# A mixture of experts after an attention block: expert outputs added straight into the output tensor, gates gathered with the rows

## The reference

```python
mod = (silu(c) @ wmod).reshape(4, 6, 1, -1)
sa, ca, ga, sb, cb, gb = (mod[:, i] for i in range(6))
ga = (2*(ga >= 0) - 1) * maximum(abs(ga), 0.25)      # gates, one row of 256 per sequence
gb = (2*(gb >= 0) - 1) * maximum(abs(gb), 0.25)
x = x + ga * attention(layernorm(x) * (1 + ca) + sa)  # 16 query heads, 4 key/value heads of 16
h = layernorm(x) * (1 + cb) + sb
x = x + gb * experts(h)
# experts: probs = softmax(h @ router.T); of 8 experts a token keeps the likeliest ones up to
# a total of 0.9; out = sum over kept e of w[e] * ((silu(h @ gate[e].T) * (h @ up[e].T)) @ down[e].T)
```

## Time and profile before

| | us |
|---|---|
| median of 3 runs (613.22, 614.0, 616.6) | 614.0 |
| the profiled execution, its own time | 614.37 |
| its span, first to last instruction | 612.6 |
| PE busy | 483.4 (79%) |
| DVE busy | 371.3 (61%) |
| ACT busy | 282.5 (46%) |
| POOL busy | 170.9 (28%) |
| mean granted clock of TensorE | 0.894 of full speed |

### The profile page before, as it was taken

The page is one execution under the profiler, slowest core; times in us unless marked ns, Lnnn a source line. Parts: engine busy times, 40 slices in busy tenths (PEclk is TensorE's granted clock), DMA queues, the critical chain, the costliest instruction groups (busy, mean ns, idle before and its releaser), DMA issues. The chain is left out here.

```text
span 612.6 us, 10534 instructions
## 1 busy us (share of the span) xinstructions
PE 483.4 (79%) x3498; PEld 351.2 (57%) x3499; DVE 371.3 (61%) x910; ACT 282.5 (46%) x409; POOL 170.9 (28%) x184
## 2 busy tenths in 40 slices
PE   2745978898899789997315599999997998999810
PEld 2333323244344433425215599999997998999810
DVE  4496287669936983567678175665643755465526
ACT  0244669776886788782000244453423543443300
POOL 6104000000000000000000336656665556476440
PEclk9965989998999999987655699999998998999975
DMA  8243100000000010010121134636453446333338
GB/s 291 95 135 117 61 1 1 1 0 2 24 13 1 1 35 1 1 35 1 34 73 35 46 104 98 158 60 164 90 125 61 109 98 151 56 52 60 44 37 271
DMA packets 33815, 42.01 MB, mean 69 GB/s; under 512 B 5620, under 2 KB 26868, under 8 KB 33784
## 3 DMA queue, kind: packets, MB, share of 16 engines
q0 software_dynamic: 10400, 16.22, 14.5%
q1 hardware_dynamic: 23384, 25.39, 13.0%
HBM read 28.14 MB, written 13.46 MB: 68 GB/s over the span
## 5 line engine op out<-in xcount | busy, mean ns | idle before, releaser
L511 ACT ACTIVATE probs<-psS 128x1024 f32<-128x1024 f32 x128 | 124.0, 1023 | 16.3 <-PE psS L1162 16.0
L1340 PE MATMUL psS<-hs_hi,w_hi 128*128 128x256 f32 x400 | 117.5, 294 | 6.9 <-issue 3.9
L1340 PE MATMUL psS<-hs_lo,w_hi 128*128 128x256 f32 x400 | 114.4, 286 | 0.0
L1340 PE MATMUL psS<-hs_hi,w_lo 128*128 128x256 f32 x400 | 114.3, 286 | 0.0
L404 POOL DMA_INDIRECT y_rows<-y_sel,idx_out x50 | 83.4, 1668 | 55.3 <-DVE y_sel L1035 45.0
L1340 PEld LDWEIGHTS psS<-hs_hi,w_hi 128*128 128x128 f32 x400 | 77.5, 194 | 8.4 <-issue 7.7
L1162 PE MATMUL psS<-qT,kT 96*128 96x512 bf16 x256 | 71.7, 393 | 11.1 <-ACT probs L511 9.4
L1340 PEld LDWEIGHTS psS<-hs_lo,w_hi 128*128 128x128 f32 x400 | 77.7, 194 | 0.0
L1340 PEld LDWEIGHTS psS<-hs_hi,w_lo 128*128 128x128 f32 x400 | 77.5, 194 | 0.0
L1271 PE MATMUL psY<-probs,v_aug 128*32 128x512 f32 x512 | 70.8, 626 | 0.0
L369 POOL TENSOR_TENSOR rstd<-var_eps,minus_half 128x4 f32<-128x4 f32 x4 | 4.8, 1195 | 235.2 <-DVE var_eps L764 235.2
(11 more groups left out here) (188 smaller groups left out, 807.6 us busy)
## 6 DMA issues: line engine op xcount, KB each, us to landing
w_in<-gateT SPq DMA_DIRECT2D x8, 512.0 KB
w_in<-upT SPq DMA_DIRECT2D x8, 512.0 KB
w_in<-downT SPq DMA_DIRECT2D x8, 512.0 KB
x_all<-x SPq DMA_DIRECT2D x4, 512.0 KB, 7.9
mod_rows<-mod_table SPq DMA_DIRECT2D x4, 512.0 KB, 7.6
y_rows<-zeros POOLq DMA_DIRECT2D x2, 1024.0 KB
h_rows<-h_nat SPq DMA_DIRECT2D x4, 512.0 KB, 3.0
y_all<-y_rows SPq DMA_DIRECT2D x4, 512.0 KB, 5.7
```

The lines of the kernel that those rows point to most:

```text
L511: act.activation(probs[:, gk % 4, 2 * pair:2 * pair + 2, :], psS[:, pair, :, :], ACT.Exp, scale=ATT_SCALE).then_inc(probs_done, 1)
L1340: mm = pe.matmul(ps[:, i * SW:(i + 1) * SW], w, v[:, k, :], start=at == 0, stop=at == 3 * KC - 1)
```

## The change

- The experts' results are added (scattered) into `out` itself. Therefore SP writes each sequence's `x` after attention into `out` as soon as it stands, behind the write of `h`, and the read-back, the product with `gb`, the sum and the final write at the end are gone, as is the zeroing of `y_rows`.
- The gate `gb` has to be applied before the scatter: `h_rows` gets 256 more numbers per row (520 in all), into which POOL writes the gate rows with four transfers as soon as they are made. A gather brings them along, `take_weights` copies 2x264 numbers instead of 2x8 into a ring of four buffers, and `output` multiplies by weight and gate row in one instruction. `modulate_gates(1)` moves from the end to the end of DVE's body 0.
- Lists are filled with tokens that did not choose the expert (their weight is 0) instead of pad rows: three small operations more in the rank, two fewer after the lists, and no pad rows.
- POOL makes the roots for sequences 2 to 4 first and the routing tables after them. PE waits at its first score for a semaphore of its own (`v_ones`), and the waits for all constants move behind attention.

```diff
@@ sync
                 sp.dma_start(h_rows[bass.ds(b * N, N), 0:C]...).then_inc(h_out, 16)
+                sp.dma_start(out_rows[bass.ds(b * N, N), :].rearrange("(t p) c -> p t c", p=P),
+                             x_all[:, bass.ds(b * TT, TT), :]).then_inc(x2_out, 16)
...
-            sp.wait_ge(scattered, ZEROING + 32 * items)
-            for b in range(B):
-                sp.dma_start(y_all[:, b * TT:(b + 1) * TT, :],
-                             y_rows[b * N:(b + 1) * N, :].rearrange("(t p) c -> p t c", p=P)).then_inc(y_in[b], 16)
-            for b in range(B):
-                sp.wait_ge(out_ready, b + 1)
-                sp.dma_start(out[b].rearrange("(t p) c -> p t c", p=P), ...).then_inc(y_out, 16)
+            sp.wait_ge(x2_out, 16 * B)
+            sp.wait_ge(scattered, GATES + 32 * items)
@@ gpsimd
-            for m, v in ((v_aug[...], 0.0), (tie, 1.0), (earlier, 1.0), (zeros, 0.0)): memset
+            pool.memset(v_aug[:, :, :, :, D:YROWS], 0.0).then_inc(zeroed, 1)
+            pool.wait_ge(zeroed, 4)
+            pool.memset(v_aug[:, :, :, :, D:D + 1], 1.0).then_inc(v_ones, 1)
+            pool.wait_ge(ln1_eps, 2)
+            pool.tensor_tensor(rstd1[:, TT:], var_eps1[:, TT:], minus_half[:, 0:NT - TT], ALU.pow).then_inc(ln1_rstd, 1)
...          memsets, affine_selects, iota slot_row, slot_tile, token (0-based); no pad_row
-            pool.wait_ge(ln1_eps, 2)
-            pool.tensor_tensor(rstd1[:, TT:], ...)
-            for r0, r1 in ((0, T // 2), (T // 2, T), (T, T + PADS)): zeros to y_rows; zeros to h_rows
+            pool.wait_ge(modr_done, 3)
+            for b in range(B):
+                pool.dma_start(h_rows[b * N:(b + 1) * N, C + E:ROW].rearrange("(t p) c -> p t c", p=P),
+                               mod_rows[:, B + b:B + b + 1, :].broadcast_to([P, TT, C])).then_inc(scattered, 16)
...
-                    pool.indirect_dma_start(y_rows[:, :], ..., y_sel[:, k, :], None, compute_op=ALU.add)
+                    pool.indirect_dma_start(out_rows[:, :], ..., y_sel[:, k, :], None, compute_op=ALU.add)
@@ vector, end of body 0
                     modulate_gates(0, xhat[:, :, :], h_nat[:, :, :])
+                    dve.wait_ge(modr_done, 1)
+                    modulate_gates(1, xhat[:, :, :], h_nat[:, :, :])
                     dve.tensor_scalar(mod_rows[:, SCALE_ROW:, :], ..., 1.0, None, ALU.add).then_inc(modr_done, 1)
@@ vector, routing
+            dve.tensor_copy(token_f[:, :, :], token[:, :, :]).then_inc(token_ready, 1)
...
-            step(dve.tensor_copy(rank_i[:, :, :], rank[:, :, :]))
+            step(dve.tensor_tensor(others[:, :, :], token_f[:, :, :], wide, ALU.add))
+            step(dve.scalar_tensor_tensor(out=others, in0=rank, scalar=-2.0, in1=others, op0=ALU.mult, op1=ALU.add))
+            step(dve.scalar_tensor_tensor(out=others, in0=keep, scalar=0.0, in1=others, op0=ALU.is_equal, op1=ALU.mult))
+            step(dve.tensor_tensor(rank_i[:, :, :], rank[:, :, :], others[:, :, :], ALU.add))
...
-            step(dve.tensor_copy(row_f, row_i)); step(row_f = (row_f + 1) * keep); step(row_h = row_f - 1)
+            step(dve.tensor_copy(row_h[:, :, :], row_i[:, :, :].rearrange("p t e -> p e t")))
...
-            step(is_pad = (lists == 0) * pads); ids_i = lists - 1 + is_pad; idx_all = pad_row - 1
+            dve.tensor_copy(ids_i[:, :, :], lists).then_inc(rt_step, 1)
+            dve.memset(idx_all[:, :], 0).then_inc(idx_ready, 1)
@@ vector, experts
-                dve.tensor_scalar(w_sel[:, bass.ds(m + 1, 1), :, 1:]..., h_sel[:, :, C:ROW], 0.0, None, ALU.max)
+                dve.tensor_scalar(sel[:, bass.ds(m % RING, 1), :, 1:]..., h_sel[:, :, C:ROW], 0.0, None, ALU.add)
...
-                    weighed = dve.tensor_scalar(y_sel[:, k, :], psY[:, k, 0:C], w_sel[...], None, ALU.mult)
+                    weighed = dve.scalar_tensor_tensor(out=y_sel[:, k, :], in0=psY[:, k, 0:C], scalar=row[:, bass.ds(e1, 1)],
+                                                       in1=row[:, 1 + E:], op0=ALU.mult, op1=ALU.mult)
...
-            modulate_gates(1, ...), and for each b: y = y * gate rows (L1072), y = y + x_all (L1074)
```

More of the change, by code:

```diff
@@ L942, in _ @@
             step(dve.tensor_tensor(rank[:, 1:, :], rank[:, 1:, :], total[:, 0:NT - 1, :], ALU.add))
[L943 removed]
+            wide = total[:, NT - 1:NT, :].broadcast_to([P, NT, E])
+            step(dve.tensor_tensor(others[:, :, :], token_f[:, :, :], wide, ALU.add))
+            step(dve.scalar_tensor_tensor(out=others[:, :, :], in0=rank[:, :, :], scalar=-2.0, in1=others[:, :, :],
+                                          op0=ALU.mult, op1=ALU.add))
+            step(dve.scalar_tensor_tensor(out=others[:, :, :], in0=keep[:, :, :], scalar=0.0, in1=others[:, :, :],
+                                          op0=ALU.is_equal, op1=ALU.mult))
+            step(dve.tensor_tensor(rank_i[:, :, :], rank[:, :, :], others[:, :, :], ALU.add))
             step(dve.tensor_scalar(tile_i[:, :, :], rank_i[:, :, :], 7, None, ALU.logical_shift_right))
@@ L946, in _ @@
             step(dve.tensor_copy(tile_h[:, :, :], tile_i[:, :, :]))
-            step(dve.tensor_copy(row_f[:, :, :], row_i[:, :, :]))
-            step(dve.scalar_tensor_tensor(out=row_f[:, :, :], in0=row_f[:, :, :], scalar=1.0, in1=keep[:, :, :],
-                                          op0=ALU.add, op1=ALU.mult))
-            step(dve.tensor_scalar(row_h[:, :, :], row_f[:, :, :].rearrange("p t e -> p e t"), -1.0, None, ALU.add))
+            step(dve.tensor_copy(row_h[:, :, :], row_i[:, :, :].rearrange("p t e -> p e t")))
             dve.wait_ge(h_out, 16 * (B + 1))
@@ L1013, in take_weights @@
                 dve.wait_ge(gathered, 32 * (m + 1))
-                dve.tensor_scalar(w_sel[:, bass.ds(m + 1, 1), :, 1:].rearrange("p o k e -> p (o k) e"), h_sel[:, :, C:ROW], 0.0,
-                                  None, ALU.max).then_inc(w_copied, 1)
+                dve.tensor_scalar(sel[:, bass.ds(m % RING, 1), :, 1:].rearrange("p o k e -> p (o k) e"), h_sel[:, :, C:ROW], 0.0,
+                                  None, ALU.add).then_inc(w_copied, 1)
             def product(m, h):
@@ L1064, in _ @@
             output(E, items - 1)
-            modulate_gates(1, y_all[:, 0:B, :], y_all[:, B:2 * B, :])
-            dve.wait_ge(modr_done, 3)
-            for b in range(B):
-                y, tiles = y_all[:, b * TT:(b + 1) * TT, :], slice(b * TT, (b + 1) * TT)
-                dve.wait_ge(y_in[b], 16)
-                dve.tensor_tensor(y, y, mod_rows[:, B + b:B + b + 1, :].broadcast_to([P, TT, C]), ALU.mult).then_inc(out_step, 1)
-                dve.wait_ge(out_step, b + 1)
-                dve.tensor_tensor(y, y, x_all[:, tiles, :], ALU.add).then_inc(out_ready, 1)
         @block.tensor
```

96 lines of the change are left out of this document (37 added, 59 removed).

## The result

| | before | after |
|---|---|---|
| median of 7 runs each, same chip | 614.6 | 617.8 |
| range | 613.2 to 616.6 | 617.0 to 620.6 |
| profiled execution: its time, its span | 614.4, 612.6 | 618.0, 616.3 |

The ratio is 1.0059, 95% interval 1.0035 to 1.0084: slower by 0.6%, where 601 was forecast. The span is 16.7 us longer than the 599.6 of the sum. Differences between two changed kernels go across chips, on which the kernel before had medians of 614.2 to 615.3; they are good to about 1 us.

What follows compares the result with a forecast made beforehand. PE, nearly always busy in attention and experts, was taken as the bound. End -17.8, start -5.4, gates +5.4, routing +0.3 and experts +4.5 sum to -13.0: span 599.6, median 601 us, range 593 to 610.

Steps and rivals of the forecast that it cites:

- Start, -5.4: Setup: with the tables later, xhat of sequence 1 saves PE 5.8 us; holding sequence 2's xhat costs 0.4.
- Gates, +5.4: DVE's body 0: modulate_gates(1) ahead of normalise_x(2) delays PE by 3.7 us, plus 1.7 for a lower clock.
- Routing +0.3: Routing: three more small operations before the lists, two fewer behind, two fewer in the middle, one copy; net +0.3 us.
- The experts, +4.5: Expert turns: longer gathered rows land later, costing seven tight turns and the first gather; +4.5 us in all.
- The landing: Expert gathers: twice the bytes per row add up to 0.5 us to each landing.
- may hold [the scatter's issue] a little, 0 to 0.3: Experts: the longer take_weights on DVE falls beside POOL's scatter issue and may hold it 0 to 0.3 us.
- What takes the place of the end, +0.2: End of program: after the last scatter only SP's wait for it and one semaphore remain, 0.2 us.
- 1: Whole kernel: the terms hold as summed, 601 us, own range 597 to 606; chance 0.60.
- 5, the other side: Experts: a longer gather issue on POOL sets every item's pace; 613.5 us, or 629 with contention; chance 0.08.
- the danger sign: Experts: PE's waits at h_sel summing to more than 10 us would show the prediction wrong.

Runs made afterwards that it cites:

- `gates_early`: Changed kernel with both modulate_gates and the 1 + scale moved up in DVE's body 0 to right behind normalise_x(1); 608.7 us, ratio 0.9879.
- `copy16`: Changed kernel, gathers of 520 numbers kept, but take_weights copies only 2x8 weights and output uses sequence 0's gate row; 608.6 us, ratio 0.9894.
- `short16`: Changed kernel with gathered rows of 264 numbers, take_weights copying 2x8, and output using sequence 0's gate row; 602.1 us, ratio 0.9798.
- `copy528`: Changed kernel, long rows and 2x264 copy kept, but output multiplies by sequence 0's gate row at a fixed address; 610.5 us, ratio 0.9927.
- `sem_nudge`: Changed kernel with two increments of an unused semaphore on DVE ahead of the first operation of split_weights; 613.8 us, ratio 0.9998.
- `tail`: Changed kernel with POOL's loop running as many turns as there are items, without empty turns; 610.0 us, ratio 0.9928.

## Why the prediction was wrong

- **Start, -5.4:** right (5.3 ahead at PE's first transposes and again from 67 to 104).
- **Gates, +5.4:** right where it was summed. The wait (+4.1) and the half clock behind it made 5.6: the lead of 5.3 was a lag of 0.3 at 152. Another 1.7 came where I did not look, from 3.4 us more at 1.2 GHz at 262. `gates_early` gives both back.
- **Routing +0.3:** the operations that the prediction lists cancel (four more, four fewer), so its sum did not follow from them; the lag grew by 0.4 from 268 to the first list. Lists and `out` as the target: too small to see.
- **The experts, +4.5: the step that failed.** Measured are 13.5 in the turns and 0.8 ahead of them. I had PE's waits at `h_sel` grow by the later landing alone, and let the other engines' order stand. In all 16 profiles the turns last 222.5 to 224.2 us, plus PE's waits at `h_sel`, plus half of the time at 1.2 GHz between the first turn and the last (an estimate from those three rows of each profile); from before to after the waits grow by 10.7 and the half clock by 2.2. Behind that stand three things.
  - The landing: taken as 0.5 later per gather, measured 0.7 to 0.9. Its cost, 4.9 to 6.5 us by `copy16` against `short16`, is near the whole term as summed, which is partly luck: the sum has 6 in the turns for a landing 0.8 later. As an estimate by the Trainium skill (DMA: Bandwidth & Descriptors, Anatomy of one DMA), 131 KB more would have made the landing 0.3 later; the measurement decides.
  - The wide copy: 1.9 in the medians when the rows are long, nothing when they are short.
  - The tie of scatter and split, in no case of mine. `copy528` is 7.3 faster than the changed kernel, but it also takes register operations out of `output`; `sem_nudge` keeps them, has no long issue either, and is 4.1 faster. In the profiles both shorten the turns by 5.5 to 5.7. So the tie costs 4 to 7 us, and where the medians of these two part is open. I wrote that `take_weights` "may hold [the scatter's issue] a little, 0 to 0.3", and looked at durations only. The starts in the trace of before are 0.03 us apart and 0.08 away from the bad side, so any edit to `output` or to POOL's turn could tip the order. The change tipped it with an operand's address.
- **What takes the place of the end, +0.2: failed as well, 4.7 measured.** I took the end of the work for the end of the program. POOL's seven empty turns and the drain were in the trace of before, hidden beneath the 17 us that the change removes; asking what else still ran beneath that stretch would have found them.
- **The cases:** 1 had the right list but not these two; 5, the other side, had the wrong mechanism (the issue of the gather, 1.0 us as before), though its place, the gather's round ahead of the turn, was where the time went. What I called the danger sign, waits at `h_sel` above 10 us, came: 14.0.

What can be tested of the sum: 601 + 4.5 (end) + 0.4 (landing) + 2.1 (up to the first list) = 608.0, and `copy16`, which has these and neither the wide copy nor a long issue, takes 608.6. From there to 617.8 the steps of 1.9 (wide copy) and 7.3 are differences of medians and add up by construction. Shown by experiments: the end, the gates, the landing, the tie as a cause, and that an operand's address tips it. Only argued: the exact size of the tie, whether the wide copy costs 2 us with long rows (the interval of `copy528` overlaps that of `copy16`) and why, and what in DVE's register operations moves by 0.05 us.

## What to carry to other kernels

When an edit removes the last stretch of a program, look at what every other engine's stream still does there, its loops' empty turns and its drain too. Where two engines that disturb each other start within some 0.1 us in the trace, treat their order as a coin: give the loss a chance of its own, and separate them by a wait or by another order of the work. And a wait that ends at a transfer has several releasers in a row (scatter ahead of the gather, then the copy behind the split): moving the first alone gained 2.6 us beside the end's 4.2, moving the second as well gained 13 more.

## What the hardware showed that I had not expected

- A scatter issue (128 rows) that begins 0.046 to 1.02 us behind the start of a DVE tensor_tensor of 128x1024 with both inputs in SBUF (1.23 us) ends 2.72 to 2.74 us after that start (16 of 16); beginning at 0.043 or less, it takes 1.62 (56 of 56). The Trainium skill (SBUF — State Buffer, Who interferes with whom) has it that a DVE operation with two SBUF inputs contends with GpSimd's reads, but infers that building DMA descriptors is not stalled by tensor_tensor; here the issue of an indirect scatter is.
- Doubling a gathered row to 2080 bytes makes its landing 0.7 to 0.9 us later where no other transfer runs.
- POOL's drain ends 0.3 to 0.4 us behind the landing of its last indirect transfer when it begins ahead of that (5.5 us in `tail`), and takes 1.7 to 1.9 us when it begins after it (changed kernel, kernel before).
- An operation at a fixed address instead of one in a register moved DVE against POOL by 0.05 us at every second change of expert, worth 4 to 7 us here.
